# A four-layer transformer: the last attention's last two head groups batch by batch, with the last mixture's norm, routing and row scatters in their slots

## The chip, the cores and the metric

The kernel runs on one core of a Trainium2 chip. The time is device microseconds of one execution, the median over the runs. A core has TensorE (matmuls and transposes into PSUM), VectorE, ScalarE and GpSimd, which work on SBUF and PSUM, and SyncE (SP), which here only issues DMAs. Each engine runs its own instructions in order; semaphores order them between engines.

## The reference, cut to what matters

The input is 8 batches of 256 tokens with 256 features in fp32. Four layers of attention and feed-forward follow each other, each behind a layer norm and added to x. The change touches the last layer and the place where its buffers are blanked.

```python
x = x + L3_attn(layernorm(x))    # 16 heads: 128 plain + 64 rotated dims, v 128 wide, no mask
x = x + L3_ffn(layernorm(x))

def L3_ffn(x):                                   # T = 2048 tokens, 32 experts, 6 a token
    scores = sigmoid(x @ gate_w)
    group_scores = max(scores.reshape(T, 4, 8), axis=-1)
    masked = where(in the 2 best groups, -inf, scores)
    selected = top_k(masked, 6)
    weights = scores[selected] / sum(scores[selected])
    expert_out = sum over selected e of weights[e] * (silu(x @ w_gate[e]) * (x @ w_up[e])) @ w_down[e]
    shared = (silu(x @ sw_gate) * (x @ sw_up)) @ sw_down       # hidden width 352
    return expert_out + shared                   # w_gate, w_up: 256 x 176, w_down: 176 x 256
```

## The kernel before, in words

x lies in SBUF as 16 tiles of 128 tokens. The layers are stages one after the other; at the end of a stage all engines meet at a barrier and the stage's buffers are freed. Nothing of a later stage starts before it.

**The last attention** (`wide_attention_stage`) works through 8 groups of two heads. In a group it goes over the 8 batches; a `Unit` is one batch of one group and has two slots, one for each head. In a slot TensorE does projections of the next unit (`piece`, L609), the product with the values of the slot before (`value`, L694), the transposes of its own probabilities (`transposed`, L677, into bank 4), the next slot's scores (L647 rotated, L667 plain) and the output projection of the slot before (`output`, L609), which VectorE adds to x (L872). Products run as three passes over a high and a low part. ScalarE writes the high part of a result (L739, L765, L770, and `halves` L746), VectorE the low part (L808, L853, L858, L879), which TensorE waits for. The rotated half goes through `turned` (VectorE, L817), a sum on GpSimd (L895), `halves`, and eight DMAs on SP's queue. ScalarE's exponentials (L757) wait for VectorE's maximum (L847) and reciprocal (L866). The order of these steps on each engine is that of `over_slots`. As the groups are the outer loop, every batch of x is complete only at the end of the stage.

**The last mixture** (`sparse_stage`) norms and transposes all of x (`norm_stage`), computes the logits of all tokens, chooses six experts a token on VectorE (MAX8 and MATCH_REPLACE, L2080 and L2084), counts the tokens of each expert and gives each chosen pair a slot in a table in HBM, dense, each expert's part rounded up to tiles of 128. 96 indirect DMAs of GpSimd (L2241, 16 tiles x 6) scatter the normed rows, with gates and token number, into this table; it was filled with blanks by a DMA in the second narrow attention (`write_blanks`), long before. In the meantime TensorE computes the shared expert (L1959, L1969) in four chunks of tokens. Expert weights are 19.9 MB in SBUF; the buffers of routing and of the shared expert lie in their last part, so 22 of 32 experts are loaded at the start and the rest when the shared expert and the four quarters of the scatters are done (L1895, L1899). Then SP loads the 127 tiles of the table (L1904), through a ring of 12 buffers, which a buffer rejoins when the tile's result was added. For each tile TensorE transposes the rows (L1981), multiplies (L1992, L2000, L2009), ScalarE scales by the gates (L2059) and GpSimd adds the rows to one of two sums in HBM with an indirect DMA (L2248). At the end the sums are added to x and written out.

## Time and profile before

| | |
|---|---|
| Median of 3 runs | 3108.55 us (3105.43 to 3110.13) |
| Span of the profiled execution, first to last instruction | 3056.3 us |
| Its own time beyond the span | not stated by the page |
| TensorE busy | 2599.8 us, 85% |
| VectorE busy | 1932.4 us, 63% |
| ScalarE busy | 1548.7 us, 51% |
| GpSimd busy | 911.9 us, 30% |
| TensorE's mean granted clock | 0.904 of full |

The page counts an engine as busy while an instruction executes; waits and DMA issues aren't in it. Its second section cuts the span into 40 slices, which tell the stages apart; its fourth follows the work that ended last back to what released it. The runs' time and the span differ by 52.3 us, which lie before the first and after the last instruction. The last two groups of the last attention run from about 2338 to 2540 us, the last mixture from there to the end.

### The profile page before, as it was taken

The page shows a single profiled execution, that of the slowest core. Times are in us where ns is not written, and L with a number is a line of the kernel's source. Part 1 is how long each engine was busy: PE and PEld are TensorE (multiplying, and loading weights), DVE is VectorE, ACT ScalarE, POOL GpSimd, SP SyncE. Part 2 cuts the span into 40 slices and gives each one's busy share as a digit, 9 for nine tenths or more (in the row PEclk, how much of TensorE's full clock was granted, in tenths as well). Part 3 has the DMA queues.
Part 4 walks back from the last instruction along what each step waited for, and adds up shares of the span by engine and source line. Part 5 has one row for each costly group of instructions (what it writes and reads, how often), then busy time and mean ns, then how long its engine had stood idle before and what let it go on. Part 6 is the DMA issues. An engine that isn't in the chain of part 4 may idle for free. (4 is left out here: it accounts for less than half of the span.)

```text
span 3056.3 us, 64440 instructions
## 1 busy us (share of the span) xinstructions
PE 2599.8 (85%) x19761; PEld 2186.9 (72%) x19763; DVE 1932.4 (63%) x5973; ACT 1548.7 (51%) x4641; POOL 911.9 (30%) x804
## 2 busy tenths in 40 slices
PE   6984985799986799999968499999999995659996
PEld 5662553566664699999946499999999993337774
DVE  5667323678874788788843577777777775125554
ACT  5875221799985555555543344544444544013332
POOL 2111785210102322222235311111111112756664
PEclk8995755899997899999979799999999997879998
DMA  6003555910001111011025333332333225467676
GB/s 192 2 2 132 89 93 115 342 39 2 2 2 45 69 35 53 31 56 35 21 111 164 122 108 101 100 97 87 104 106 100 83 84 231 156 188 122 119 122 156
DMA packets 191749, 291.70 MB, mean 95 GB/s; under 512 B 30464, under 2 KB 158776, under 8 KB 188704
## 3 DMA queue, kind: packets, MB, share of 16 engines
q1 hardware_dynamic: 152544, 226.20, 23.1%
q0 software_dynamic: 38976, 62.68, 10.5%
q8 instruction: 116, 1.90, 0.3%
q14 instruction: 113, 0.93, 0.1%
HBM read 110.68 MB, written 94.22 MB: 67 GB/s over the span
## 5 line engine op out<-in xcount | busy, mean ns | idle before, releaser
L609 PE MATMUL bank<-norm_t_high,w 128*128 128x256 f32 (+1 forms) x2176 | 446.4, 287 | 8.3 <-DVE w L791 8.3
L757 ACT ACTIVATE probs<-bank,neg_max 128x256 f32<-128x256 f32 (+1 forms) x512 | 224.5, 443 | 396.8 <-DVE inv L866 387.6
L609 PEld LDWEIGHTS bank<-norm_t_high,w 128*128 128x128 f32 x2176 | 363.1, 194 | 9.0 <-issue 9.0
L1175 ACT ACTIVATE probs<-neg_scores,bound 128x256 f32<-128x256 f32 (+1 forms) x768 | 367.0, 487 | 3.1 <-DVE bound L1246 2.6
L609 PE MATMUL bank<-norm_t_low,w 128*128 128x256 f32 (+1 forms) x1088 | 309.9, 285 | 0.0
L1246 DVE CUSTOM_DVE_ANT_0 neg_scores<-bank,table 128x256 f32<-128x256 f32 (+1 forms) x768 | 261.7, 397 | 63.0 <-PE bank L1087 63.0
L895 POOL TENSOR_TENSOR summed<-turned 128x512 f32<-128x512 f32 x64 | 82.5, 1290 | 711.9 <-DVE turned L817 711.9
L667 PE MATMUL bank<-k,q 128*128 128x256 f32 (+1 forms) x1536 | 245.2, 296 | 0.0
L765 ACT ACTIVATE probs_t<-bank 128x384 fp32r<-128x384 f32 (+1 forms) x256 | 139.5, 545 | 200.9 <-PE bank L677 200.5
L872 DVE SCALAR_TENSOR_TENSOR x_sb<-bank,inv,x_sb 128x256 f32 (+1 forms) x512 | 224.3, 479 | 24.1 <-DVE inv L866 13.6
L2248 POOL DMA_INDIRECT sums<-shared,norm_t x127 | 198.1, 1560 | 136.3 <-ACT shared L2059 67.7
L609 PE MATMUL bank<-w,out_t 128*128 128x256 f32 x1536 | 227.0, 283 | 10.4 <-DVE out_t L858 10.2
L694 PE MATMUL bank<-probs_t,v 128*128 128x256 f32 (+1 forms) x1536 | 218.7, 278 | 1.8 <-DVE probs_t L853 1.6
L609 PEld LDWEIGHTS bank<-w,out_t 128*128 128x128 f32 x1536 | 201.5, 190 | 14.1 <-DVE out_t L858 11.2
L609 PEld LDWEIGHTS bank<-norm_t_low,w 128*128 128x128 f32 x1088 | 211.0, 194 | 0.0
L1992 PE MATMUL bank<-weights,x_t 128*128 x696 | 207.9, 422 | 3.6 <-issue 1.5
L1099 PE MATMUL bank<-ident_sb,probs 128*128 128x128 f32 x1408 | 193.9, 279 | 12.4 <-ACT probs_t L1182 12.1
L667 PEld LDWEIGHTS bank<-k,q 128*128 128x128 f32 x1536 | 197.1, 191 | 10.2 <-issue 0.2
L694 PEld LDWEIGHTS bank<-probs_t,v 128*128 128x128 f32 x1536 | 199.2, 190 | 4.1 <-DVE probs_t L853 3.6
L1099 PEld LDWEIGHTS bank<-ident_sb,probs 128*128 128x128 f32 x1408 | 156.3, 142 | 57.8 <-issue 29.9
L1283 POOL TENSOR_SCALAR k_placed<-k_t,place 128x512 f32<-128x512 f32 x48 | 74.3, 1563 | 387.5 <-ACT k_t L1149 387.5
L1254 DVE COPY probs_t<-bank 128x512 f32<-128x512 f32 (+1 forms) x192 | 123.5, 643 | 80.9 <-PE bank L1099 80.3
(404 smaller groups left out, 5957.7 us busy)
## 6 DMA issues: line engine op xcount, KB each, us to landing
z<-norm_t_high SPq DMA_DIRECT2D x96, 256.0 KB, 2.5
z<-norm_t_low SPq DMA_DIRECT2D x96, 256.0 KB, 2.5
rows<-blank SPq DMA_DIRECT2D x1, 21336.0 KB, 64.9
norm_t<-rows SPq DMA_DIRECT2D x127, 168.0 KB, 2.6
q_turned<-halves SPq DMA_DIRECT2D x256, 64.0 KB
k_turned<-halves SPq DMA_DIRECT2D x256, 64.0 KB
staged<-in_attention SPq DMA_DIRECT2D x12, 1280.0 KB, 6.6
weights<-in_experts SPq DMA_DIRECT2D x1, 13376.0 KB, 37.6
```

Of the source, the lines that this page charges most:

```text
L609: ins = nc.tensor.matmul(out, stationary(a), moving(c), start=(kt == 0 and m == 0), stop=(kt == n - 1 and m == 2))
L667: ins = nc.tensor.matmul(s[:, score_columns(causal, t)], qq[a][:, j, t * P:(t + 1) * P], kk[c][:, kj, 0:width], start=False, stop=(n == 2 ...
L694: ins = nc.tensor.matmul(o_bank[:, to], vv[a][:, kt, jv * P:(jv + 1) * P], pp[c][:, of], start=(kt == 0 and n == 0), stop=(kt == QT - 1 an ...
L757: ins = nc.scalar.activation(probs[j % 2][:, t, 0:width], s_bank[j % 2][:, score_columns(causal, t)], ACT.Exp, bias=neg_max[j % 2][:, t:t ...
L765: nc.scalar.activation(probs_t[j % 2][0][:], t_bank[:, 0:NB], ACT.Copy).then_inc(t_high, 1)
L872: ins = nc.vector.scalar_tensor_tensor(tile, y_bank[j % 2][:, t * C:(t + 1) * C], inv[j % 2][:, t:t + 1], tile, ALU.mult, ALU.add)
L1099: ins = nc.tensor.transpose(t_bank[g % 2][:, at:at + P], probs[q % 2][g][:, t, kt * P:(kt + 1) * P], core.ident[:])
L1175: ins = nc.scalar.activation(probs[q % 2][g][:, t, 0:width], neg_scores[g][:, t, 0:width], ACT.Exp, bias=bound[q % 2][:, g, t:t + 1], scal ...
L1246: ins = nc.vector.tensor_tensor_reduce(out=neg_scores[g][:, t, 0:width], in0=s_bank[g][:, t * S:t * S + width], in1=table[:, at:at + width ...
L1254: nc.vector.tensor_copy(probs_t[q % 2][g][:], t_bank[1][:, 0:NB]).then_inc(t_by_dve, 1)
L1992: ins = nc.tensor.matmul(up_bank[e % 2][:, 0:COLUMNS], x_t[e % 2][:, kt, :], weights[:, kt * COLUMNS:][:, bass.ds(expert[e], COLUMNS)], st ...
L2248: nc.gpsimd.indirect_dma_start(scratch.results[e % len(scratch.results)], bass.IndirectOffsetOnAxis(ids, 0), product[e % OUT_RING], None, ...
```

## The change: what it does

The last attention goes over groups 0 to 5 as before. The last two groups run batch by batch: 16 "late" units, batch 0 in group 6, batch 0 in group 7, batch 1 in group 6, and so on, 32 slots, written out instead of looped. For this the weights of group 7 get buffers of their own and are loaded with the stage's first loads. So batch b of x is complete after slot 4b + 3.

A new class `Dispatch` does the last mixture's norm, transposes, logits, choice of experts, ranks and row scatters for one batch (2 tiles) at a time, in hooks at the begin or end of the slots that follow: for batch b statistics in slot 4b + 5, norm and transposes in 4b + 6, copy and logits in 4b + 7, the choice and the ranks in 4b + 8, the rows in 4b + 9, and three scatters in each of 4b + 9 to 4b + 12. On VectorE all hooks stand before the slot's own work, on TensorE after it. The transposes, logits and ranks use bank 4, which is the attention's bank of transposed probabilities. What batches 5 to 7 still need after slot 31 goes into the new `routed_stage`, as hooks between the steps of the shared expert.

Each expert has a fixed region of 2048 rows in the table in HBM, so a row's place needs no count of later batches. A row is 304 floats instead of 336. The table has 65,664 rows instead of 16,256 and all are blanked in the second narrow attention. A tile's place is computed from the counts and SP reads it into a register before each of the 127 loads. The ring of row buffers has 8 buffers instead of 12, that of results 6 instead of 8. 24 of 32 experts are loaded first, four when the shared expert is done, and four in three parts as the scatters are done. `shared_up`, the expert loop and the final additions are the old ones.

```diff
--- before.py
+++ after.py
...
-BLANK = 336
+BLANK = 304
...
-        staged = st.sb("staged", [P, cfg.width])
-        w = [st.sb("w", [P, cfg.width], F32R) for _ in range(2)]
+        staged = dispatch.rows_flat[:, 0:cfg.width] if dispatch else st.sb("staged", [P, cfg.width])[:]
+        w = [[st.sb("w", [P, cfg.width], F32R) for _ in range(2)] for _ in range(2 if dispatch else 1)]
...
+        LATE = G - 2 if dispatch else G
...
             def next(self):
+                if self.late is not None:
+                    return late_unit(self.late + 1)
                 if self.closes:
+                    if isinstance(self.g, int) and self.g == LATE - 1:
+                        return late_unit(0) if dispatch else None
                     return Unit(self.g + 1, 0, 0)
-                return Unit(self.g, self.i, 1) if self.parity == 0 else Unit(self.g, self.i + 1, 0)
+                u = Unit(self.g, self.i, 1) if self.parity == 0 else Unit(self.g, self.i + 1, 0)
+                u.last = not dispatch and u.closes and u.in_last_group
+                return u
...
+        def late_unit(at):
+            b, of = divmod(at, 2)
+            u = Unit(LATE, b, of)
+            u.g, u.b, u.n, u.pair = LATE + of, b, LATE * B + at, LATE * PAIRS + b
+            u.late, u.weights = at, of
+            u.opens, u.closes, u.in_last_group, u.last = at < 2, False, True, at == 2 * B - 1
+            return u
...
             group(0, first=True)
-            with eng.Fori(1, G - 1) as g:
-                group(g)
-            group(G - 1, last=True)
+            if LATE > 2:
+                with eng.Fori(1, LATE - 1) as g:
+                    group(g)
+            if LATE > 1:
+                group(LATE - 1, last=not dispatch)
+            for at in range(2 * B if dispatch else 0):
+                work(late_unit(at))
...
+                    if begin and u.late is not None:
+                        begin(u.late * HG + j)
...
+                    if end and u.late is not None:
+                        end(u.late * HG + j)
...
+        def last_parts_at(u, j):
+            if dispatch and isinstance(u.n, int) and u.n == 1:
+                return [part for part in range(NW) if part * HG // NW == j]
+            return []
...
+                    if u.late is not None:
+                        dispatch.wait_bank_read(pe, u.late * HG + j - 1)
...
+                def late_end(s):
+                    if dispatch.uses_bank(s):
+                        pe.wait_ge(t_low, LATE * B * HG + s + 1)
+                    dispatch.tensor_end(pe, s)
+                over_slots(pe, piece, value, transposed, score, output, end=late_end)
...
+                def late_begin(s):
+                    b = dispatch.batch_at(s, 1)
+                    if b is not None:
+                        dve.wait_ge(y_added, (LATE * B + 2 * b + 2) * HG)
+                    dispatch.vector_begin(dve, s)
...
+                def late_begin(s):
+                    if s == HG:
+                        pool.wait_ge(w_low, (LATE + 1) * NW)
+                        dispatch.pool_rows(pool)
+                    dispatch.pool_begin(pool, s)
...
+def write_regions(core, sp, scratch):
+    cfg = scratch.cfg
+    sp.dma_start(scratch.rows.rearrange("(i p) r -> p i r", p=P),
+                 core.blank[:, 0:cfg.row].rearrange("p (a r) -> p a r", a=1).to_broadcast([P, cfg.E * cfg.room // P + 1, cfg.row]))\
+        .then_inc(scratch.blank_rows, 16)
+    for s in scratch.results:
+        sp.dma_start(s.rearrange("(i p) c -> p i c", p=P),
+                     core.blank[:, 0:C].rearrange("p (a c) -> p a c", a=1).to_broadcast([P, TILES + 1, C])).then_inc(scratch.blank, 16)
...
+    SLOTS, SETUP = 4, 9
+    STATS, NORMED, COPIED, CHOSEN, RANKED = 1, 2, 3, 4, 5
+    TURNED, LOGITS, RANKS = 2, 3, 4
...
+    def batch_at(self, s, step):
+        b, rest = divmod(s - step, self.SLOTS)
+        return b - 1 if rest == 0 and 1 <= b <= B else None
...
+    def pool_end(self, pool, s):
+        top = self.cfg.top
+        each = QT * top // self.SLOTS
+        for part in range(self.SLOTS):
+            b = self.batch_at(s, self.RANKED + part)
+            if b is None:
+                continue
+            if b == 0 and part == 0:
+                pool.wait_ge(self.scratch.blank_rows, 16)
+                pool.wait_ge(self.scratch.blank, 16 * self.cfg.sums)
+            if part == 0:
+                pool.wait_ge(self.row_ready, b + 1)
+            for n in range(part * each, (part + 1) * each):
+                t, k = b * QT + n // top, n % top
+                self.nc.gpsimd.indirect_dma_start(self.scratch.rows, bass.IndirectOffsetOnAxis(self.slot[:, t, k:k + 1], 0),
+                                                  self.rows[:, t, :], None).then_inc(self.sent[self.sent_of(b)], 16)
...
+    def tensor_end(self, pe, s):
+        nc, bank, E = self.nc, self.bank, self.cfg.E
+        b = self.batch_at(s, self.TURNED)
+        if b is not None:
+            pe.wait_ge(self.normed, b + 1)
+            need(pe, self.ranks_read, b)
+            for t in range(QT):
+                for kt in range(KT):
+                    ins = nc.tensor.transpose(bank[:, kt * S + t * P:kt * S + (t + 1) * P],
+                                              self.rows[:, b * QT + t, kt * P:(kt + 1) * P], self.core.ident[:])
+            ins.then_inc(self.turned, 1)
+        b = self.batch_at(s, self.LOGITS)
+        if b is not None:
+            pe.wait_ge(self.copied, b + 1)
+            for t in range(QT):
+                for kt in range(KT):
+                    ins = nc.tensor.matmul(bank[:, t * E:(t + 1) * E], self.norm_kt[:, kt, (b * QT + t) * P:(b * QT + t + 1) * P],
+                                           self.router_w[:, kt, :], start=(kt == 0), stop=(kt == KT - 1))
+            ins.then_inc(self.logits_done, 1)
+        b = self.batch_at(s, self.RANKS)
+        if b is not None:
+            pe.wait_ge(self.chosen_ready, b + 1)
+            pe.wait_ge(self.logits_read, b + 1)
+            row = lambda t: t.rearrange("p t e -> p (t e)")
+            nc.tensor.matmul(bank[:, 0:QT * E], self.earlier_bf[:], row(self.chosen_bf[:]), start=True, stop=False)
+            nc.tensor.matmul(bank[:, 0:QT * E], self.ones_bf[:], row(self.seen[:, b * QT:(b + 1) * QT, :]), start=False, stop=True)\
+                .then_inc(self.ranks_done, 1)
...
+    def scalar_begin(self, act, s):
+        nc, core = self.nc, self.core
+        b = self.batch_at(s, self.NORMED)
+        if b is not None:
+            if b == 0:
+                act.wait_ge(self.setup, self.SETUP)
+            act.wait_ge(self.shift_ready, b + 1)
+            for t in (b * QT, b * QT + 1):
+                ins = nc.scalar.activation(self.rows[:, t, 0:C], core.x[:, t, :], ACT.Identity, bias=core.shift[:, t:t + 1],
+                                           scale=core.rstd[:, t:t + 1])
+            ins.then_inc(self.normed, 1)
+        b = self.batch_at(s, self.COPIED)
+        if b is not None:
+            act.wait_ge(self.turned, b + 1)
+            nc.scalar.activation(self.norm_kt[:, :, b * S:(b + 1) * S], self.bank[:].rearrange("p (k t) -> p k t", k=KT), ACT.Copy)\
+                .then_inc(self.copied, 1)
...
+    def vector_begin(self, dve, s):
+        for step, work in ((self.RANKED, self.rank), (self.STATS, self.statistics), (self.NORMED, self.shift), (self.CHOSEN, self.choose)):
+            b = self.batch_at(s, step)
+            if b is not None:
+                work(dve, b)
...
+    def pick(self, dve, values, left, chosen, n, k):
+        nc, low = self.nc, max(n, 8)
+        for t in range(QT):
+            ins = nc.vector.max(self.best[:, t, :], values[:, t, 0:low])
+        self.after(dve, ins)
+        self.after(dve, nc.vector.tensor_copy(self.best[:, :, k:8], values[:, :, low:low + 8 - k]))
+        for t in range(QT):
+            ins = nc.vector.match_replace(left[:, t, :], self.best[:, t, :], values[:, t, :], -BIG)
+        self.after(dve, ins)
+        self.after(dve, nc.vector.tensor_tensor(chosen, left[:, :, 0:n], values[:, :, 0:n], ALU.not_equal))
+    def choose(self, dve, b):
+        nc, E, N = self.nc, self.cfg.E, self.cfg.groups
+        by_group = lambda t: t.rearrange("p t (g n) -> p t g n", g=N)
+        dve.wait_ge(self.logits_done, b + 1)
+        if b == 0:
+            dve.wait_ge(self.setup, self.SETUP)
+        need(dve, self.exps_ready, b)
+        nc.vector.tensor_copy(self.logits[:], self.bank[:, 0:QT * E].rearrange("p (t e) -> p t e", t=QT)).then_inc(self.logits_read, 1)
+        dve.wait_ge(self.logits_read, b + 1)
+        self.after(dve, nc.vector.tensor_reduce(self.group_values[:, :, 0:N], by_group(self.logits[:]), AX.X, ALU.max))
+        self.pick(dve, self.group_values, self.group_left, self.group_chosen[:], N, 2)
+        self.after(dve, nc.vector.tensor_scalar(self.group_chosen[:], self.group_chosen[:], -MASKED, MASKED, ALU.mult, ALU.add))
+        self.after(dve, nc.vector.tensor_tensor(
+            by_group(self.padded[:, :, 0:E]), by_group(self.logits[:]),
+            self.group_chosen[:].rearrange("p t (g a) -> p t g a", a=1).to_broadcast([P, QT, N, E // N]), ALU.add))
+        need(dve, self.ranks_read, b)
+        self.pick(dve, self.padded, self.left, self.chosen[:], E, self.cfg.top)
+        need(dve, self.ranks_done, b)
+        ins = nc.vector.tensor_copy(self.chosen_bf[:], self.chosen[:])
+        for t in (b * QT, b * QT + 1):
+            ins = nc.vector.tensor_tensor(self.seen[:, t + 1, :], self.seen[:, t, :], self.chosen[:, t % QT, :], ALU.add)
+            if t == b * QT:
+                self.after(dve, ins)
+        ins.then_inc(self.chosen_ready, 1)
...
+        self.after(dve, nc.vector.tensor_scalar(self.exps[:], self.exps[:], 1.0, None, ALU.add))
+        dve.wait_ge(self.ranks_done, b + 1)
+        nc.vector.tensor_tensor(self.places[:], self.bank[:, 0:QT * E].rearrange("p (t e) -> p t e", t=QT),
+                                self.base[:].to_broadcast([P, QT, E]), ALU.add).then_inc(self.ranks_read, 1)
+        self.after(dve, nc.vector.reciprocal(self.exps[:].rearrange("p t e -> p (t e)"), self.exps[:].rearrange("p t e -> p (t e)")))
+        nc.vector.tensor_tensor(self.exps[:], self.chosen[:], self.exps[:], ALU.mult).then_inc(self.chain, 1)
+        self.count += 1
+        dve.wait_ge(self.ranks_read, b + 1)
+        self.after(dve, nc.vector.tensor_tensor(self.places[:], self.places[:], self.chosen[:], ALU.mult))
+        nc.vector.tensor_reduce(self.total[:], self.exps[:], AX.X, ALU.add).then_inc(self.chain, 1)
+        self.count += 1
+        for t in range(QT):
+            ins = nc.vector.max(self.best[:, t, :], self.places[:, t, :])
+        self.after(dve, ins)
+        nc.vector.reciprocal(self.inv[:], self.total[:]).then_inc(self.chain, 1)
+        self.count += 1
+        self.after(dve, nc.vector.tensor_scalar(self.slot[:, b * QT:(b + 1) * QT, :], self.best[:], -1.0, None, ALU.add))
+        nc.vector.tensor_tensor(self.rows[:, b * QT:(b + 1) * QT, C:C + E], self.exps[:], spread(self.inv[:]), ALU.mult).then_inc(self.row_ready, 1)
...
+    RING, OUT_RING = 8, 6
...
+    rows_at = E * W - TILES * ROW
+    early_weights = (rows_at // W - cfg.scratch_experts) * W
+    FIRST = B * Dispatch.SLOTS
+    LAST = FIRST + Dispatch.RANKED
...
+    def in_order(hook, up, down, count):
+        ups = [(c, k) for c in range(CHUNKS) for k in range(SB)]
+        for n, (c, k) in enumerate(ups):
+            if FIRST + n <= LAST:
+                hook(FIRST + n)
+            elif FIRST + n <= LAST + 3:
+                count(FIRST + n - LAST - 1)
+            up(c, k)
+            if k == 0 and c:
+                down(c - 1)
+        down(CHUNKS - 1)
...
+                sp.dma_start(shared[:], shared_in).then_inc(shared_loaded, 16)
+                for target, source in TABLES:
+                    sp.dma_start(target[:], source).then_inc(tables_loaded, 16)
+                load_weights(0, early_weights)
+                for part, (first, end) in enumerate(((0, B - 2), (B - 2, B - 1), (B - 1, B))):
+                    sp.wait_ge(dispatch.sent[part], 16 * QT * TOP * (end - first))
+                    load_weights(batch_rows(first), batch_rows(end))
+                sp.wait_ge(s_y_done, 2 * CHUNKS)
+                load_weights(early_weights, rows_at)
+                sp.wait_ge(expert_ready, 1)
+                for e in range(NT):
+                    if e >= RING:
+                        sp.wait_ge(added[(e - RING) % SUMS], landed(e - RING))
+                    at = sp.value_load(place_at[0:1, e:e + 1], min_val=0, max_val=E * cfg.room)
+                    sp.dma_start(tile_rows[e % RING], scratch.rows[bass.ds(at, P), :]).then_inc(row_loaded[e % RING], 16)
...
+        with ExitStack() as right:
+            rows_stack = ExitStack()
+            dispatch = Dispatch(core, routed, routed_scratch, right, rows_stack, d["router_3"], d["earlier"], d["base_3"], d["token_3"])
+            wide_attention_stage(core, wide[3], d["attention_3"], [d["rotation"]], measured=True, dispatch=dispatch)
+            core.split.close()
+            routed_stage(core, routed, dispatch, rows_stack, d["experts_3"], d["shared_3"],
+                         [d["steps_3"], d["below_3"], d["numbers_3"], d["experts_iota"]], out)
```

## Rows read from the trace of the kernel before

**Rows 1.** The page, first section: busy us, share, instructions of each engine.

```profile
PE 2599.8 (85%) x19761; PEld 2186.9 (72%) x19763; DVE 1932.4 (63%) x5973; ACT 1548.7 (51%) x4641; POOL 911.9 (30%) x804
```

**Rows 2.** Windows, last two groups: busy of each engine, clock, DMA share, GB/s.

```profile
2438.00:2463.00 25.00, 24.28 (x211) 23.63 (x210) 17.95 (x37) 11.76 (x33) 2.57 (x2) 1.00 0.30 88
...
sum 200.00, PE 191.64 PEld 184.62 DVE 144.64 ACT 95.30 POOL 19.36; mean PE 23.96 PEld 23.08 DVE 18.08 ACT 11.91 POOL 2.42
```

**Rows 3.** Timeline, between the stages: start, duration, instruction, idle before and releaser.

```profile
2539.33 0.88 DVE L872 SCALAR_TENSOR_TENSOR x_sb<-bank,inv,x_sb 128x256 f32<-128x256 f32 x2 [1.05 <-issue]
...
2541.07 0.35 SPq L182 DMA_DIRECT2D router_w<-in_router  x1
...
2580.85 16.26 PE L1959 MATMUL bank<-norm_t,shared 128*128 128x512 f32 x32
...
2640.94 5.45 PE L1969 MATMUL bank<-shared,weights 128*128 128x256 f32 x24 [0.84 <-DVE weights L2182]
...
2708.68 1.09 PE L1981 MATMUL bank<-ident_sb,norm_t 128*128 128x128 f32 x4 [62.28 <-DMA norm_t<-rows]
```

**Rows 4.** Source L2241, the row scatters: duration min/median/max, first and last start.

```profile
L2241 POOL DMA_INDIRECT rows<-weights,slot x96: 956/960/1051, 2581.2 to 2701.4; - x96
...
DMA to landing us min/median/max: 2.4/2.5/11.7
```

**Rows 5.** Expert loop: timeline, source L2248 (the additions), and windows.

```profile
2799.99 0.38 PE L1981 MATMUL bank<-ident_sb,norm_t 128*128 128x128 f32 x2
...
2801.32 1.56 POOL L2248 DMA_INDIRECT sums<-shared,norm_t  x1 [1.30 <-ACT shared L2059]
...
L2248 POOL DMA_INDIRECT sums<-shared,norm_t x40: 1556/1560/1580, 2798.5 to 2898.7; - x40
...
DMA to landing us min/median/max: 3.7/3.9/5.8
...
2800.00:2900.00 100.00, 100.00 (x484) 75.04 (x483) 50.91 (x202) 31.88 (x81) 60.57 (x40) 1.00 0.69 120
```

**Rows 6.** DMA issues: number, KB each, median us from issue to landing.

```profile
norm_t<-rows SPq DMA_DIRECT2D x127, 168.0 KB, 2.6
...
weights<-in_experts SPq DMA_DIRECT2D x1, 13376.0 KB, 37.6
...
weights<-in_experts SPq DMA_DIRECT2D x1, 3392.0 KB, 13.8
...
weights<-in_experts SPq DMA_DIRECT2D x4, 672.0 KB, 4.2
...
shared<-in_shared SPq DMA_DIRECT2D x1, 1152.0 KB, 5.1
```

**Rows 7.** Timeline, slots of the last two groups.

```profile
2439.59 0.98 PE L647 MATMUL bank<-k_turned,q_turned 64*128 64x256 f32 x12 [0.72 <-DMA k_turned<-halves]
...
2457.68 0.60 PE L677 MATMUL bank<-ident_sb,probs 128*128 128x128 f32 x4
...
2458.02 0.41 DVE L858 TENSOR_TENSOR out_t<-bank,out_t 128x256 fp32r<-128x256 f32 x1
...
2458.83 0.88 PE L609 MATMUL bank<-w,out_t 128*128 128x256 f32 x6
...
2459.43 0.69 DVE L808 TENSOR_TENSOR k<-bank,k 128x512 fp32r<-128x512 f32 x1 [1.00 <-ACT k L739]
```

**Rows 8.** Lines of VectorE by form, old routing: count, busy us, mean ns.

```profile
L2080 DVE MAX8 weights<-weights 128x8 f32<-128x32 f32 x16 | 1.6, 177 | 0.0
```

**Rows 9.** Second narrow attention: windows, and SP's timeline around the blank write.

```profile
580.00:600.00 20.00, 19.12 (x208) 14.65 (x208) 14.39 (x62) 19.33 (x71) 6.18 (x4) 1.00 1.07 362
...
620.00:640.00 20.00, 19.12 (x207) 14.53 (x205) 13.95 (x57) 18.47 (x67) 6.18 (x4) 1.00 0.01 4
...
545.83 0.38 SPq L1720 DMA_DIRECT2D rows<-blank  x1
...
919.65 0.82 SPq L182 DMA_DIRECT2D last<-x_sb  x1
```

514 lines of the change are left out of this document (469 added, 45 removed).

## The prediction

> **What bounds the kernel now.** I read the page's first section, then the stretches of the last two stages, then waits and timeline between them. TensorE is busy for 85% of the span [rows 1], but unevenly. In the last two head groups of the last attention (2338 to 2538) it is busy for 191.6 of 200 us, VectorE 144.6, ScalarE 95.3, GpSimd 19.4, at a granted clock of 1.00, which is 2.4 GHz [rows 2]: TensorE bounds it, one batch of one group takes about 12.5 us (two slots), and a batch of two groups, the unit of the change, 25 us.
> Then comes a hole. The attention's last addition to x ends at 2540.2, the shared expert's matmuls start at 2580.85 and end at 2646.4, and TensorE next starts at 2708.7 [rows 3]. It waits 62.3 us for one row load (the release is in the last row), and that waits for GpSimd: 96 row scatters, each 0.96 us and 0.30 us of issue, so 1.265 us apart, from 2581.15 to 2702.4, the last landed 2.5 us after its issue [rows 3, 4]. So 168.5 us lie between the end of attention and the first expert tile (2540.2 to 2708.7), of which 65.5 are TensorE's shared expert; the rest is norm and routing (40.6) and the scatters' tail. In the expert loop TensorE is again the bound: 100 us busy of 100, and 484 matmul records at 12 a tile make 2.49 us a tile [rows 5].
>
> **Part 1, what goes.** The norm stage, the routing of 16 tiles at once and the 96 scatters leave the path. What replaces the 168.5 us, counted from the attention's end:
> - Stage exit and the load of the shared weights. The old first DMA issue is 0.9 us after the end; the load of 1152 KB lands 5.1 us after its issue [rows 6]. TensorE starts at 6.2. Batch 6's choice of experts on VectorE (part 3: 3.0 us) hides beneath.
> - The shared expert's 65.5 us, kept from before. What the clock costs after a short pause is within the bounds.
> - TensorE's own additions in this stage, batch 6's ranks, batch 7's transposes, logits and ranks, and the counts: 1.7 + 0.5 = 2.2 us.
> - Stalls for batch 7, whose chain now hangs between the shared expert's steps in a fixed order on every engine: for its normalised rows, activation 0.6, gating 0.7, shift 0.1, two normalisations of 0.58, so 2.5 us; for the copy 1.0; for the choice of experts 4.5 (VectorE must first add the finished shared chunk, 0.7, then 3.0, and hops); the counts 1.0. Together 9. Bounds: 3 (only the choice) and 18 (double).
> - GpSimd has 27 scatters left at the stage's start (3 of batch 5, 12 each of 6 and 7). Batch 7's row is ready at about 41 us; 12 x 1.265 later it is 56, landed 59. That is before the shared expert ends at 6.2+65.5+2.2+9 = 83, so the scatters no longer count. The first weights (24 of 32 experts, 14.6 MB) land at about 45, by 37.6 us for 13.4 MB [rows 6].
> - What is late next: the weights of four experts, 2432 KB, are issued only when the shared expert is done, since its buffers lie there. Between 4.2 us (672 KB) and 13.8 us (3392 KB, beside scatters) [rows 6]; I take 9. The first row load is queued behind, 0.8. First tile at 83 + 9.8 = 92.8.
> So 168.5 becomes 93: 75.7 us gone. Bounds 64 to 84.
>
> **Part 2, what moves into the attention on TensorE.** For each batch four fp32 transposes (0.60 us for such a four [rows 7]), four logits matmuls of 32 columns (some 0.8, eight weight loads of about 0.1 bound it) and two bf16 ones (0.3): 1.7 us. TensorE has no slack there. The work runs in slots 5 to 31 of 32, 27 slots, 6.75 batches' worth: 11.5 us. This is the lower bound of the stretch.
>
> **Part 3, what moves there on the others.** VectorE per batch: two statistics of 256 columns (0.35 each by the 0.41 of a 256-wide op [rows 7]) and two aggregates (0.1 each), 1.0 with hops; shift 0.13; the choice, 18 small instructions, 0.1 to 0.2 us each (a MAX8 of 32 columns 0.18 [rows 8]), with hops 3.0; the ranks and gates, 11 such, 2.1. Together 6.2 us. It is idle 55 of 200 us, 7 per batch of 25 [rows 2], so its sum fits, barely (24.3 of 26.7). But the slack is in small pieces: its second half of the output is ready at 2458.43 and TensorE wants it at 2458.83; the idle piece of that slot is 1.0 and comes after it [rows 7]. The choice (3.0) stands at the head of a slot, before that output half. Little of it is absorbed: the stall of TensorE lies between nothing and 2.6 (3.0 less 0.4); I take 1.5, since VectorE stands idle for part of the time before the slot's first result. The slot after, with ranks and statistics (3.1), finds TensorE already late by this; I add nothing. ScalarE: two normalisations 1.15 us stand at the head of slot 2 ahead of the rope half `halves`, whose sum on GpSimd is already late by VectorE's 3.1: 1.5 us more. The bank of the transposed probabilities is shared, so in three of four slots TensorE waits for VectorE's read of it at the slot's end instead of 1.4 us later: 0.7 in all. Sum of a batch 1.7 + 1.5 + 1.5 + 0.7 = 5.4, times 6.75 = 36.5 us. If none of VectorE's idle could be used the stretch would be (1.7+6.2) x 6.75 = 53; with ScalarE's 1.15 too, 61.
> GpSimd: 12 scatters x 1.265 = 15.2 us a batch, with two rope sums (1.29) and a power of 1.2 about 19 of 30: it holds, and a rope sum finds it free since three scatters (3.8) fit in a slot of 6.25. SP's queue gets nothing in these slots; its rope moves (eight of 0.6 us and two loads a unit) already release TensorE late once by 0.72 us [rows 7], which is why I count delays of `halves`. The scatters' traffic, 1.9 MB in 30 us, adds 62 GB/s to 88 [rows 2]; 362 are seen elsewhere [rows 9], I count nothing, at most 0.5 us a batch (3 us).
> The split of the last group's weights moves from the last boundary to the second batch, same instructions: nothing, 1 us either way.
>
> **Part 4, the fixed regions.** The blank rows grow from 21.3 MB to 65,664 rows x 1216 B = 79.8 MB, with the sums' 4.5 MB 84.3 MB. At the 355 GB/s of the old write (362 GB/s in a stretch [rows 9]) it lasts 237 us from 545.8 [rows 9], to 783. The next use of SP's queue is at 919.65 and TensorE did 208 matmuls in 20 us during the write, 207 after it [rows 9]: hidden, cost nothing. Uncovered it would cost up to 170 us; it has 137 us of margin.
> In the expert loop the row ring shrinks from 12 to 8 and each load first reads its place into a register of SP, a delay x that no row shows. A tile's addition is issued 1.3 us after the transposes of four tiles later, lands 3.9 later, and the row load lands 2.6 after its issue: 7.8 + x, in the four tiles left, 9.96 us [rows 5, 6]. So x up to 2.1 is free. Below zero is excluded as it is added; above, the nearest row is the 2.5 us round trip of a scatter [rows 4], which would give (7.8+2.5)/4 = 2.58 a tile, 119 x 0.09 = 10 us. I take x below 2.1: nothing. DMA: Bandwidth & Descriptors of the Trainium skill (Latency and other measured facts) has about 600 ns as the floor of such a load, which by this sum would be free too; no run so far shows it.
>
> **Sum.** The time from the attention's end shrinks by 75.7, the attention grows by 36.5: 39 us. The page states only a span, 3056.3; it becomes 3017. The median of the runs is 52.3 above that span; I leave this margin unchanged: 3108.55 - 39 = 3070.
>
> **Rivals.**
> *All but TensorE's own work is covered* (VectorE's 7 us of idle a batch speak for it, the 0.4 us of slack against): stretch 11.5, 3108.55 - 75.7 + 11.5 = 3044. 0.15.
> *VectorE and ScalarE serialise with TensorE*: stretch 53 to 61, 3086 to 3094. 0.15. Even this is faster, which is what makes the sign fairly safe: to lose, a batch has to grow by 75.7/6.75 = 11.2 us, twice my sum.
> *The ring of 8 bounds the loop*: x = 3.5 gives 11.3/4 = 2.83 a tile, 40 us, 3110, no change. Against it: SP is idle most of each tile. 0.08, most of it a small excess.
> *GpSimd is the bound in attention* (the other side). It issues in order, so a rope sum waits behind three scatters and TensorE behind the sum. If GpSimd could work only while VectorE doesn't, 72% of the time taken, a scatter takes 0.96/0.28 + 0.30 = 3.7 us, and a batch 12 x 3.7 + 3.8 = 48 instead of 30.4: 18 x 6.75 = 122 us, 3192. It decides from a scatter pitch of (30.4-3.8)/12 = 2.2 us and turns the sign at 2.7. Against it: forty additions of the loop took 1556 to 1580 ns with VectorE half busy [rows 5]; an exclusion would scatter them. 0.04.
> The skill's SBUF — State Buffer (SBUF: two separate sides) states the rule behind this one: a VectorE copy in its two-port mode locks GpSimd out of writing descriptors, a DMA of 0.62 us taking 3.1. At a pitch of 3.1 the same sum gives 41 us a batch and 3142. The even 1556 to 1580 ns speak against it for the operand kinds of this kernel.
> *The rest*, such as a stall that spans the new stage boundary: 0.03.
>
> **Numbers.** Forecast 3070, 0.55. A change under 0.2% (6 us) can't be told from none. Faster holds the forecast, both stretch cases and most of the ring's: 0.88; same 0.03; slower 0.09. Range: 3044 at the covered end, to 3098 at the serialised end with 4 us for the loop; a bit under it on the low side for a shorter part 1: 3040 to 3098.
>
> **What would show it.** Scatter records in the attention, 0.96 us each, the last about 56 us after its end. TensorE's 62.3 us wait is replaced by one of about 10 us for the last weights. The late batches 30.4 us apart instead of 25, with waits of TensorE on VectorE's output half and on rope moves. Loop at 2.49 us a tile. Wrong if the late batch is over 36 us, if a tile takes over 2.55, or if the stage between takes over 104 us.

## The result and the profile after

The changed kernel took 3053.3 us (3051.7 to 3054.6, 4 runs) beside 3108.5 (3105.4 to 3110.1) for the kernel before: ratio 0.9823, 95% interval 0.9809 to 0.9837, 55 us less. The forecast was 3070. The trace shown of the kernel before has a span of 3056.3 us, that of the changed one 3051.2 with a time of 3053.0. So the spans differ by 5 us and the times by 55: the rest of 52.3 us that the prediction carried over is gone. This turned out to be the main question.

The page's first lines, after [rows 1]:

```profile
span 3051.2 us, 64760 instructions
...
PE 2616.4 (86%) x19821; PEld 2198.8 (72%) x19821; DVE 1956.0 (64%) x6103; ACT 1547.1 (51%) x4636; POOL 918.8 (30%) x820
```

Windows of the last attention's late part, the stage between, and the expert loop (us, then busy us of PE, PEld, DVE, ACT, POOL, granted clock, DMA share, GB/s):

```profile
2348.00:2607.00 259.00, 216.96 (x1718) 206.41 (x1717) 179.26 (x527) 105.73 (x281) 95.32 (x100) 0.93 0.32 103
2607.00:2704.00 97.00, 70.90 (x214) 39.90 (x215) 29.47 (x110) 13.11 (x20) 26.99 (x29) 0.87 0.67 268
2704.00:3025.00 321.00, 320.33 (x1524) 238.31 (x1522) 160.65 (x635) 100.14 (x253) 193.62 (x125) 0.99 0.67 112
```

The late part took 259 us where [rows 2] had 200, at a granted clock of 0.93 instead of 1.00. TensorE's timeline in the stage between, against [rows 3]:

```profile
2605.27 1.65 PE L664 MATMUL bank<-w,out_t 128*128 128x256 f32 x6 [0.93 <-DVE out_t L932]
2613.01 0.24 PE L2535 MATMUL bank<-chosen_bf,earlier_bf 128*128 128x64 bf16 x1 [6.09 <-DVE seen L2622]
2613.06 0.24 PE L2536 MATMUL bank<-seen,ones_bf 128*128 128x64 bf16 x1
2614.11 9.13 PE L2805 MATMUL bank<-norm_ffn,shared 128*128 128x512 f32 x16 [0.81 <-DMA shared<-in_shared]
2626.28 0.66 PE L2519 MATMUL bank<-ident_sb,rows 128*128 128x128 f32 x4 [3.04 <-ACT rows L2547]
...
2646.54 0.23 PE L2535 MATMUL bank<-chosen_bf,earlier_bf 128*128 128x64 bf16 x1 [6.67 <-DVE seen L2622]
...
2689.42 5.45 PE L2816 MATMUL bank<-shared,weights 128*128 128x256 f32 x24 [0.84 <-DVE weights L2933]
2703.61 1.09 PE L2828 MATMUL bank<-ident_sb,norm_ffn 128*128 128x128 f32 x4 [8.74 <-DMA norm_ffn<-rows]
```

Seen from TensorE, the stage now takes 96.7 us (2606.9 to 2703.6). The wait of 62.28 us in [rows 3] has become one of 8.74, for the last weights and the first row. The blank write and the loop's row loads (the page's DMA issues: number, KB each, median us to landing; then the source view of the places that SyncE reads):

```profile
rows<-blank SPq DMA_DIRECT2D x1, 77976.0 KB, 241.2
...
norm_ffn<-rows SPq DMA_DIRECT2D x127, 152.0 KB, 2.6
...
L2764 SPq TENSOR_LOAD <-place_at x127: 262/267/502, 2695.3 to 3013.3; - x127
```

What the prediction did not have stands in the late slots. Timeline of TensorE and ScalarE, then of GpSimd with its six scatters:

```profile
2434.70 0.60 PE L734 MATMUL bank<-ident_sb,probs 128*128 128x128 f32 x4
...
2439.70 0.60 ACT L832 ACTIVATE probs_t<-bank 128x512 fp32r<-128x512 f32 x1 [5.65 <-remote]
...
2442.16 0.24 PE L2535 MATMUL bank<-chosen_bf,earlier_bf 128*128 128x64 bf16 x1 [4.34 <-DVE probs_t L927]
...
2430.87 0.99 POOL L2508 DMA_INDIRECT rows<-rows,slot  x1 [0.16 <-issue]
2432.17 0.96 POOL L2508 DMA_INDIRECT rows<-rows,slot  x1 [0.30 <-issue]
...
2437.24 0.96 POOL L2508 DMA_INDIRECT rows<-rows,slot  x1 [0.30 <-issue]
```

```profile
2436.00:2441.00 5.00, 0.98 (x7) 0.77 (x6) 0.98 (x3) 1.09 (x2) 1.89 (x2) 0.97 0.56 175
2441.00:2447.00 6.00, 4.84 (x24) 4.84 (x25) 5.32 (x19) 2.15 (x7) 0.00 (x0) 0.50 0.34 111
```

### The profile page after: what moved, and what is told of

The parts are those of the page before. It is cut to its first block and busy times, and to the rows that moved or that the text cites. A ratio compares the mean times of both kernels' runs of the same rounds, so it can differ in the third digit from the quotient of the medians.

```text
span 3051.2 us, 64760 instructions
## 1 busy us (share of the span) xinstructions
PE 2616.4 (86%) x19821; PEld 2198.8 (72%) x19821; DVE 1956.0 (64%) x6103; ACT 1547.1 (51%) x4636; POOL 918.8 (30%) x820
## 5 line engine op out<-in xcount | busy, mean ns | idle before, releaser
L832 ACT ACTIVATE probs_t<-bank 128x384 fp32r<-128x384 f32 (+1 forms) x256 | 139.7, 546 | 218.6 <-PE bank L734 193.4
L2986 POOL DMA_INDIRECT sums<-norm_ffn x127 | 197.4, 1554 | 161.5 <-ACT norm_ffn L2885 148.1
L946 DVE SCALAR_TENSOR_TENSOR x_sb<-bank,inv,x_sb 128x256 f32<-128x256 f32 (+1 forms) x512 | 224.3, 480 | 24.2 <-DVE inv L940 11.3
L2839 PE MATMUL bank<-weights,shared 128*128 x508 | 174.5, 467 | 0.7 <-issue 0.3
```

Source lines behind the costliest of these rows:

```text
L832: nc.scalar.activation(probs_t[j % 2][0][:], t_bank[:, 0:NB], ACT.Copy).then_inc(t_high, 1)
L946: ins = nc.vector.scalar_tensor_tensor(tile, y_bank[j % 2][:, t * C:(t + 1) * C], inv[j % 2][:, t:t + 1], tile, ALU.mult, ALU.add)
L2839: ins = nc.tensor.matmul(up_bank[e % 2][:, 0:COLUMNS], x_t[e % 2][:, kt, :], weights[:, kt * COLUMNS:][:, bass.ds(expert[e], COLUMNS)], st ...
L2986: nc.gpsimd.indirect_dma_start(scratch.results[e % SUMS], bass.IndirectOffsetOnAxis(ids, 0), product[e % OUT_RING], None, compute_op=ALU.a ...
```

## The experiments

In all, the kernel before was timed in six comparisons. Four gave 3108.5, 3107.5, 3113.8 and 3117.2 us, two gave 3049.6 and 3054.2; inside one comparison it spreads by 15 us at most (3043.4 to 3058.1). Each comparison ran on one chip, so I speak of chips of two kinds, **slow-scatter** and **plain**. The five chips on record (the first comparison's isn't) were each used for one comparison only, so whether the kind belongs to the chip or to the occasion is not shown. The shown trace of the kernel before, 3056.3, is of a plain one, by its stages.

**The kernel before again (plain chip).**

> The kernel before, unchanged. Its profiled span was 3056.3 us with a time of 3108.6, a rest of 52.3 us; after the change span and time differ by 1.8 us. Theory A: the rest is real and belongs to the kernel before (span again 3056, time 3108): the change took 50 us away outside the span. Theory B: the trace that was shown of the kernel before leaves some 50 us out, or is of an execution faster than the timed ones: then the span now lies within 2 us of its time, near 3106, and the 50 us are to be found inside the span.

Span 3046.1 with a time of 3047.9; 3052.9 us over 8 runs. On each of the eight the span is 1.7 to 1.9 us under the time. Theory A, a real rest outside the span, fell. B held in that span and time agree, but not in its 3106 us, and this chip could not show the 50 us.

**The kernel before a third time (slow-scatter chip).**

> The kernel before took 3107.5 us on the chip of the first comparison and of the ring experiment, 3049.6 us on the chip of the no-scatters experiment; its shown trace of 3056.3 us is of the second kind. If this call falls on the first kind: span 3101 to 3108, and the 50 us lie where GpSimd's scatters run. Theory C: completions of TensorE come up to 5 us late while row scatters are in flight, and in the kernel before that delays the 96 row scatters' stage (168.5 us in the shown trace) and the expert loop: the stage between grows to 185 to 200 us, the loop takes the rest. Rival: the 50 us are spread over all stages in proportion (1.7% of each). If it falls on the second kind: 3044 to 3055, as before.

3116.2 us over 8 runs, span 3110.1. Windows of routing and row stage of the second layer's mixture, last two groups, stage between, loop; first here, then in the trace of the plain chip:

```profile
1543.00:1704.00 161.00, 112.30 (x567) 78.74 (x565) 55.78 (x221) 61.64 (x149) 74.44 (x78) 0.86 0.38 132
2354.00:2552.00 198.00, 190.36 (x1622) 183.37 (x1618) 142.85 (x293) 93.84 (x259) 19.37 (x15) 1.00 0.29 86
2552.00:2764.00 212.00, 86.33 (x249) 47.31 (x250) 44.97 (x219) 28.57 (x52) 97.41 (x105) 0.70 0.47 181
2764.00:3084.00 320.00, 319.33 (x1524) 238.28 (x1524) 160.66 (x635) 100.41 (x254) 193.93 (x125) 0.99 0.68 118
```

```profile
1540.00:1681.00 141.00, 107.51 (x560) 77.14 (x559) 56.17 (x218) 61.35 (x144) 73.06 (x76) 0.88 0.40 138
2332.00:2533.00 201.00, 192.06 (x1622) 184.94 (x1622) 143.33 (x294) 93.79 (x259) 19.37 (x15) 0.99 0.29 85
2533.00:2701.00 168.00, 77.01 (x250) 44.39 (x252) 45.04 (x219) 28.68 (x52) 97.16 (x105) 0.72 0.59 229
2701.00:3020.00 319.00, 318.83 (x1523) 237.84 (x1523) 160.50 (x635) 99.77 (x253) 193.41 (x124) 0.99 0.68 118
```

The same instructions, the same attention and loop; only the two stages that scatter whole rows differ, by 18 us (from the first routing product to the last tile 154.4 against 136.7) and 44 us. Inside the second, VectorE (which waits for TensorE) and TensorE:

```profile
2619.26 0.69 DVE L2190 TENSOR_TENSOR x_sb<-bank,x_sb 128x512 f32<-128x512 f32 x1 [10.57 <-remote]
2650.74 0.69 DVE L2190 TENSOR_TENSOR x_sb<-bank,x_sb 128x512 f32<-128x512 f32 x1 [30.79 <-remote]
2673.22 0.69 DVE L2182 TENSOR_TENSOR weights<-weights,bank 128x512 f32<-128x512 f32 x1 [21.78 <-remote]
```

```profile
2612.91 7.03 PE L1959 MATMUL bank<-norm_t,shared 128*128 128x512 f32 x16
2673.96 5.61 PE L1959 MATMUL bank<-norm_t,shared 128*128 128x512 f32 x8 [54.02 <-issue]
2696.36 8.08 PE L1969 MATMUL bank<-shared,weights 128*128 128x256 f32 x24 [16.79 <-issue]
```

While 96 scatters follow each other from 2592.2 to 2712.7, at the usual 1.27 us, TensorE's completions come out tens of microseconds late and TensorE stands still for 54 and then 17 us. Theory C names the right stage, though its size was short (212 us, expected 185 to 200), and it fails for the expert loop, where single scatters of 1024-byte rows cost nothing (319.5 us here, 319.7 on the plain chip). The proportional rival fell. The shared expert, hidden under the scatters on a plain chip, ends at 2751 here, 38 us after the last scatter's start.

**The changed kernel again, three times (slow-scatter chips each time).**

> The changed kernel, unchanged. The kernel before took 3108.5 us beside its first timing and 3049.6 us beside the four kernels of the last experiments, a difference larger than the effect to be explained. Theory A (the gain belongs to the kernels): beside a kernel before of 3050 us the changed one takes 2995 to 3010. Theory B (the kernel before alone is disturbed in the first timing by something that its trace of 3056.3 us does not hold; stage by stage the change gives back nearly what it takes): the changed kernel takes 3045 to 3060 again, ratio 1.00. If completions of TensorE come late again while six row scatters run, it is the program's; if not, it was that chip's.

> The changed kernel, unchanged, beside the kernel before on the same chip. On the first kind of chip (before 3107): 3050 again. On the second kind (before 3050): by the forecast's terms, 39 us less than before, 3005 to 3020, with batches of the late order at 30 to 32 us and no late completions of TensorE; the rival is that the changed kernel is the same on both kinds, 3050, and the change gives nothing there.

> The changed kernel, unchanged. The kernel before has two times, by chip: near 3050 (row scatters leave TensorE alone) and near 3107 to 3114 (TensorE stops for 54 us and 17 us while 96 row scatters run). If the kernel before is near 3050 here: by the forecast's terms, in which scatters cost TensorE nothing, the changed kernel takes 3005 to 3030 and a batch of the late order 30 to 32 us; rival, that the change gives nothing on such a chip: 3045 or more. If it is near 3110: 3050 to 3065 again.

3050.3 us, ratio 0.983 (0.9805 to 0.9855); 3064.7, 0.9841 (0.9813 to 0.987); 3069.6, 0.9846 (0.9827 to 0.9866). The gain is 48 to 57 us on such chips, and late completions recur each time. The last two are 15 and 5 us above what was expected for such a chip (3050, and 3065 at most). None of these chips is plain, so the changed kernel itself was never timed on one, and theory A of the first of the three stays untested.

**Without the scatters of the attention's slots (plain chips, both times).** In each slot below 32; SyncE's wait for these scatters is lowered to match:

```
-            for n in range(part * each, (part + 1) * each):
+            for n in range(part * each, (part + 1) * each) if s >= B * self.SLOTS else ():
```

> Of the last mixture's 96 row scatters the 69 to be issued inside the attention are left out (their rows are never written, so the result lacks them); all other instructions stay. The attention's last two groups took 260 us instead of 199, forecast was 236. Theory 1 (scatters hold TensorE's completions back: semaphore increments of TensorE arrived up to 4.8 us after their matmuls, always when a run of six scatters ended): the 260 us become 232 to 240, the late increments are gone, the run ends 20 to 28 us earlier (3025 to 3033). Theory 2 (the wait of the ranks product for the choice in the same slot): the stretch stays at 255 us or more and the run within 5 us of 3053.

> As the earlier kernel without scatters: the 69 row scatters of the attention's slots are left out, the result lacks them. Beside a kernel before of 3050 it took 3012.5, with 29.2 us for a batch of the late order. Beside a kernel before of 3107 to 3117 the changed kernel takes 34.5 to 35 us a batch and TensorE's completions come up to 5 us late. If the scatters are the agent, the batch is 29 to 30 us here too, no completion inside the attention is more than 1 us late, and the run is 25 to 45 us under the changed kernel's 3050 to 3070. If such a chip holds TensorE back for another reason, and the scatters only coincide, the batch stays over 32 us and completions still come late.

3012.5 beside 3049.6, and 3015.5 beside 3054.2. The late part takes 224 and 226 us, 29.2 a batch, and no completion is late. Theory 2's numbers (255 us, 3053) did not come; the first run went beyond theory 1's (224 us for 232 to 240, 3012.5 for 3025 to 3033), and the second's batch of 29 to 30 us without late increments came out. But both prove less than they seem to, since these chips are plain, and a plain chip shows no late completion with scatters either (below): what was to be tested, this kernel on a slow-scatter chip, has not been run. That the scatters are the agent there rests on the times of the increments.

**Ranks one slot later.**

```
-    STATS, NORMED, COPIED, CHOSEN, RANKED = 1, 2, 3, 4, 5
-    TURNED, LOGITS, RANKS = 2, 3, 4
+    STATS, NORMED, COPIED, CHOSEN, RANKED = 1, 2, 3, 4, 6
+    TURNED, LOGITS, RANKS = 2, 3, 5
```

> The product that counts ranks, its reading and the scatters come one slot later (RANKS 5, RANKED 6). Theory 2 (TensorE's 19.2 us of waits ahead of that product are waits for the choice in the same slot): they go, the 260 us become 240 to 245 and the run 3034 to 3040. Theory 1 (completions held back by scatters): the wait is only passed on to the next product, the stretch stays at 255 us or more, the run within 5 us of 3053.

> Ranks one slot later, which beside a kernel before of 3050 took 3023. Beside 3050 again: 3020 to 3026, 3 to 12 us under the changed kernel if the wait for the choice in the same slot was worth 1.5 us a batch, none if it was not. Beside 3110: the scatters hold TensorE's completions back for as long as before, but its wait for the choice is gone; 10 us under the changed kernel if the two waits add, level or above it if the hold decides.

Plain chip: 3023.1 beside 3049.6, ratio 0.990 (0.9871 to 0.9929). Slow-scatter chip: 3061.7 (3060.9 to 3070.1) beside 3117.2, and 3069.6 (3066.8 to 3072.4) for the changed kernel. The same kernel's late part on the first and on the second:

```profile
2341.00:2577.00 236.00, 208.73 (x1707) 198.50 (x1706) 178.99 (x527) 105.02 (x281) 91.76 (x97) 0.97 0.34 110
```

```profile
2356.00:2620.00 264.00, 224.29 (x1710) 212.35 (x1706) 180.39 (x527) 105.49 (x281) 92.28 (x97) 0.90 0.31 99
```

And who waited there, ScalarE (us in total, times, longest), plain chip, then slow-scatter chip:

```profile
ACT probs L824 <- DVE inv L940: 69.0, 29, 4.1
ACT probs_t L832 <- PE bank L734: 27.1, 22, 1.5
```

```profile
ACT probs_t L832 <- PE bank L734: 20.6, 19, 1.9
ACT out_t L837 <- DMA products<-shared,norm_t: 16.8, 5, 3.7
ACT probs_t L832 <- remote: 10.9, 6, 2.8
```

With scatters in it, the plain chip has no late completion at all; of this one stage 28 us go with the kind of chip. The 236 us and 3023 us lie below both theories' numbers, which had been set from the first trace, of the other kind. (The second row there names a DMA; its time is again that of a late increment of TensorE.) On the slow-scatter chip the wait for the choice in the attention was passed on, as theory 1 said (264 us against 260 for the changed kernel beside it), but the stage between fell from 98.3 to 93.5 us, mostly because TensorE's wait for batch 7's choice ahead of L2535, 6.67 us in the first trace and 5.31 in the changed kernel's on this chip, became 1.38. The two spans are 10 us apart: 4.8 in this stage, 7.6 ahead of the late part, where the two kernels have the same instructions, while the late part grew by 3. The ranges of the times overlap, too, so that it beats the changed kernel is likely and not shown. TensorE's row with the 1.38:

```profile
2662.63 0.20 PE L2535 MATMUL bank<-chosen_bf,earlier_bf 128*128 128x64 bf16 x1 [1.38 <-DVE seen L2622]
```

**The choice in two parts**, groups at the head of slot 4 and experts at the head of slot 5 (slow-scatter chip):

```
+    STATS, NORMED, COPIED, CHOSEN, PICKED, RANKED = 1, 2, 3, 4, 5, 6
+    TURNED, LOGITS, RANKS = 2, 3, 5
...
+                           (self.PICKED, self.choose_experts)):
...
+    def choose_experts(self, dve, b):
+        nc, E = self.nc, self.cfg.E
         need(dve, self.ranks_read, b)
         self.pick(dve, self.padded, self.left, self.chosen[:], E, self.cfg.top)
```

> Ranks one slot later, and the choice in two parts: groups at the head of slot 4, experts at the head of slot 5. Theory 3 (VectorE's choice in one piece at the slot's head, 3 us, is what delays TensorE's next products): a batch of the late order takes 29 to 30 us instead of 31.1, the run is 8 to 15 us under the 3023.1 us of ranks later alone. Rival (VectorE's total work decides, or the scatters): within 4 us of 3023.

3067.9 us (3056.7 to 3070.5) beside 3050.3 for the changed kernel: ratio 0.9865 to before. The late part grew from 252 to 259 us and the stage between from 98 to 102. Theory 3's numbers were set for a plain chip, and ranks later alone was not timed on this one, so what the split itself costs is open; nothing here speaks for theory 3.

**All hooks behind the attention**, the late order kept (plain chip):

```
-                    if end and u.late is not None:
-                        end(u.late * HG + j)
...
+                for s in range(FIRST):
+                    hook(s)
                 in_order(hook, shared_activate, lambda c: None, lambda n: None)
```

> The last two groups go batch by batch as now, but every hook of the mixture (norm, routing, scatters) that stood in their slots runs behind the attention, ahead of the shared expert. Forecast's view (the order by itself costs nothing, all of the longer stretch is the hooks'): the last two groups take 199 to 202 us as before. Rival (the order costs by itself, with two sets of weights and later z loads): 210 us or more. The hooks in a row behind it are a chain through four engines: 27 slots of 5 to 9 us and 12 scatters of 1.27 us a batch, so 130 to 240 us more between the stages; the run ends at 3120 to 3230.

```profile
2340.00:2535.00 195.00, 189.11 (x1618) 182.55 (x1614) 139.51 (x288) 91.50 (x254) 19.61 (x17) 1.00 0.28 81
2535.00:2733.00 198.00, 95.72 (x308) 59.11 (x308) 69.83 (x349) 26.46 (x47) 100.22 (x112) 0.68 0.48 184
```

The late part took 195 us: the order by itself costs nothing, the whole stretch is the hooks'. The stage between took 198.6, 102 us more than the 96.7 of the first trace and 105 more than the 93.3 with ranks later on a plain chip; I had expected 130 to 240. 3082.3 us, ratio 1.0094 (1.0064 to 1.0123), where 3120 was the least expected. So on a plain chip moving the routing out of the slots makes the change a loss.

**A ring of 6 rows (slow-scatter chip).**

```
-    RING, OUT_RING = 8, 6
+    RING, OUT_RING = 6, 6
```

> The last loop's ring of rows has 6 places instead of 8. By the forecast's formula, ring times period = 4 periods + 7.8 us + what SyncE's read of a place adds (at most 2.1 us): a period of 3.9 to 4.95 us where the ring binds, so the loop of 127 tiles grows from 318 us to 495 to 630 and the run by 180 to 310 us. If reading a place adds nothing and row loads land in 3.7 us, the low end. Rival (rows come free earlier than counted): under 3.5 us a tile.

3280 us, 230 more than the changed kernel on this chip, as expected (180 to 310). The loop and SyncE's waits:

```profile
2708.00:3265.00 557.00, 427.56 (x1524) 288.45 (x1524) 160.57 (x635) 99.89 (x253) 193.81 (x125) 0.82 0.39 65
```

```profile
SPq L2764 <- DMA sums<-norm_ffn: 266.1, 99, 15.5
```

557 / 127 = 4.39 us a tile. By 6p = 4p + 7.8 + x, x is 0.98 us. With 8 places the ring would then bind at (7.8 + 0.98) / 4 = 2.2 us, under TensorE's 2.49: free, with a margin of 0.3 us a tile.

## Why the prediction came out as it did

The time, its sign and its mechanism in the main were right, and the gain was 16 us larger than forecast (55 for 39). The time fell within 17 us of the forecast partly by luck: two errors, of 40 and 24 us, met.

**The sum's transfer to the runs failed.** "The median of the runs is 52.3 above that span; I leave this margin unchanged" took it for something outside the span. On every run whose span is known it is 1.7 to 2.4 us. The 50 us were inside, in the two row stages, on chips where TensorE's completions come late beside the scatters; the trace came from another kind of chip. A rest of 52 us between span and time was itself a warning that trace and times did not belong together, and the prediction only restated it.

**Part 1, the stage between.** Forecast 168.5 to 93. From TensorE's last to its first matmul it went from 169.4 in the shown trace, but 212.4 on a chip like the timed one, to 96.7. So the forecast of what replaces it was right to 4 us and the gain was 116 instead of 76. Its parts: entry 7.2 (forecast 6.2; the shared weights set it, batch 6's choice ended 1.1 us earlier), waits for batch 7 3.04 + 6.67 = 9.7 (forecast 9), last weights and first row 8.74 (forecast 9.8), last scatter issued 63 us after the attention's end (forecast 56) and not decisive.

**Part 2, TensorE's additions.** Forecast 11.5 us. Where scatters do not disturb, TensorE's busy time of the late part is 207.1 us (the trace without scatters below) against 192.1 in the same stage of the kernel before, on plain chips: 15.

```profile
2340.00:2566.00 226.00, 207.07 (x1715) 195.32 (x1713) 177.93 (x526) 105.63 (x281) 26.08 (x31) 0.99 0.24 70
```

**Part 3, the stretch.** Forecast 36.5. On a plain chip, with ranks later: 236.2 against 200.2 in the kernel before, 36, and 30.8 us a batch against 30.4. Without scatters 24 to 26. So the size agrees for the kind of chip of the trace, but partly by luck: that is not the changed kernel, and it has a wait of its own. One slot later, the ranks stand ahead of the next batch's shift on VectorE, and ScalarE waits for the shift ahead of its rope half, 2.1 us a batch (waits from 2360 to 2605, us in total, times, longest; the longest of the second row lies behind the attention):

```profile
PE bank L664 <- DVE out_t L932: 16.4, 13, 2.3
ACT rows L2547 <- DVE shift L2587: 16.7, 7, 4.2
```

Without scatters and with the ranks in their old slot these are 9.4 to 10.3 us (in 13) and at most 3.4. Which part of the 10 to 12 us between the stretches is the scatters', which the prediction put at nothing, and which the ranks' new place, is not separated; so the changed kernel's stretch on a plain chip is open. On the timed kind it was 61 in the first run (258.8 against 197.7 to 198.2) and 54 to 73 in the others. That is the value of the rival "serialise" (53 to 61), but not its mechanism: VectorE's busy time grew by 36 us, 5.3 a batch (forecast 6.2), and it still idles 80 of 259 us; TensorE waited for increments that came late. Its "wrong if": the late batch was to stay under 36 us; in the first trace it was 33.8 to 37.5, and in the second of its three repeats 37.4 to 37.7 from the fourth batch on, so on such chips this sign of being wrong was met. Of what I named, TensorE's waits for the output half are there (the first row above, 2.4 us a batch; forecast 1.5; the kernel before has 1.2 us in all). None is put down to rope moves; ahead of the rotated scores (L702) TensorE waits 6.5 us in 7, two of them for `turned`, five with no releaser named.

**Part 4.** The write of the blank rows took 241 us (forecast 237 with the sums), and stayed hidden: SyncE's next issue is at 916.12, before at 919.65 [rows 9]. The ring of 8 does not bind: 321.5 us for 127 tiles are 2.53 a tile with both ends, against 2.52 before, and x is 0.98. (484 records at 12 a tile make 2.48 us, not 2.49, which changes nothing.) The read of a place shows as 0.27 us of SyncE in the trace, and from its start to the issue of the row load pass 0.71 us, so most of x is there. DMA: Bandwidth & Descriptors of the Trainium skill (Latency and other measured facts) gives 600 ns as a floor for such a read; the record here is below that, so the measurement decides, though all that x holds together is more.

**The rivals.** GpSimd as the bound fell: in the late slots the scatters stay at 959/963/1432 ns, 1.27 apart, with VectorE at 24 of 34 us. The rule of the Trainium skill's SBUF — State Buffer (SBUF: two separate sides) did not come to bear with that: no lock-out of descriptors is to be seen. "All covered" (11.5) fell: even without scatters the stretch is 24. The ring fell.

**Balance on slow-scatter chips**, kernel before's third run against the changed kernel's first: stage between 212.4 to 96.7, -115.7; late part 197.7 to 258.8, +61.1; loop +2.0; what comes before the late part -5.8 (two chips; the second layer's mixture, from the first routing product to the last tile, 154.4 and 149.3 us); end -0.3. Together -58.7; spans 3110.1 and 3051.2. On one chip, with the second of the changed kernel's repeats: -113.3, +73.0, +1.2, -1.8, -2.5, together -43.4, spans 43.6 apart. On a plain chip, ranks later against before: -75, +36, +2, and +9 ahead of the late part: 27.7 us of span, 26.5 of time. The +9 is spread of the same instructions: the shown trace of the kernel before starts its late part at 2341.1, this kernel at 2341.2, the other trace of the kernel before at 2332.3. By the interval the gain there is 22 to 39 us, so the forecast's 39 is at its edge and likely too large; with ranks later, the nearest kernel timed there, the gain is half of that on the other kind (55.5).

## What to carry to other kernels

Compare a trace's span with the times before using it: here a gap of 1.7% meant that it showed another kind of chip, and one of the two stages where they differed was the one that the change shortens. Scatters of whole rows look cheap in GpSimd's own records, and on some chips TensorE stands still while they are in flight; ask what else runs then, and time on more than one chip. On a plain chip, hooks moved into a TensorE-bound loop cost about what the forecast's slot-by-slot sum gave. A product that waits for a choice made in its own slot is worth trying a slot later: behind the attention that took 4 us off its wait.

## What the runs showed of the hardware

On four comparisons of six, TensorE's semaphore increments came 1 to 5 us late while about six row scatters (128 rows of 1216 bytes, 1.27 us apart) were in flight, and tens of microseconds late under 96 of them (1344 bytes); the increments then came out 0.07 us apart. Rows of 1024 bytes, one scatter per 2.5 us, delayed none. Scatter records (0.96 us) and the packets of their rows (222 ns mean on both kinds, for 5376 bytes) have the same length on both kinds, so nothing on GpSimd's side gives it away.

The semaphore events tell the two kinds apart. In the six traces of plain chips every instruction of TensorE, VectorE and ScalarE that raises a semaphore has its event within 0.05 us of its end. In the eight of slow-scatter chips 173 to 209 of TensorE's some 3,500 have none within 0.1 us, because it is late or missing, and the same holds for 144 to 173 of VectorE's 3,800 to 3,900 and 86 to 156 of ScalarE's 2,600; all of GpSimd's are there. In three of these traces (the changed kernel's first and last, the kernel before's), cut into stretches of 50 us, they lie only where GpSimd issues indirect DMAs, in the expert loops too.

That the scatters cause the delay is argued from these times; leaving them out was tried on plain chips alone. Why some chips do it, whether the recording of the events takes part, and whether it is the number in flight or the bytes, is open.
